# A state-space scan whose skip term is added by TensorE through a diagonal matrix, and gated while it is read from PSUM

## What is computed

```python
xz = x @ in_proj_w
x_in, z = jnp.split(xz, 2, axis=-1)
xc = silu(conv1d(x_in, conv_w) + conv_b)            # u of the scan
dt = softplus(ssm_out[..., -1:] @ dt_w + dt_b)
dA = jnp.minimum(jnp.exp(delta[..., None] * A), 1.0)
dBu = delta[..., None] * Bm[:, :, None, :] * u[..., None]
...
yk = (states * Ck[:, :, None, :]).sum(-1)           # sum over the 16 states
...
return y + u * Dp[None, None, :]                    # the skip term
...
return y * jax.nn.silu(z) @ out_proj_w              # the gate, then the projection
```

## Time and profile before

| | us |
|---|---|
| median of 3 runs | 1558.58 (1555.74, 1558.58, 1558.62) |
| the profiled execution | 1558.36 |
| its span | 1556.6 |
| PE busy | 1307.7 (84%) |
| weight loads on PE busy | 506.7 (33%) |
| VectorE (DVE) busy | 1243.2 (80%) |
| ScalarE (ACT) busy | 1039.3 (67%) |
| GpSimd (POOL) busy | 661.3 (42%) |

### The profile page before, as it was taken

How to read it: one execution, slowest core, us unless ns; L and a number is a source line. 1 busy time by engine, 2 the same in 40 slices (tenths; PEclk the granted TensorE clock), 3 DMA queues, 4 the chain that set the end, 5 groups by cost and what they waited for, 6 DMA issues and landing times.

```text
span 1556.6 us, 22553 instructions
## 1 busy us (share of the span) xinstructions
PE 1307.7 (84%) x8408; PEld 506.7 (33%) x8408; DVE 1243.2 (80%) x1491; ACT 1039.3 (67%) x1821; POOL 661.3 (42%) x609
## 2 busy tenths in 40 slices
PE   4365659976985897888569999999999999999998
PEld 1111224433433343333212222222222222235963
DVE  0889988999899786456679999999999999943522
ACT  3542357755853663445239998999899988997653
POOL 0678867986787684744503112111111113111430
PEclk9666789997996998999759999999999999999999
DMA  7122213322321221223212011100010000000210
GB/s 219 66 65 81 68 49 96 88 69 75 81 75 54 81 75 31 55 68 50 33 54 50 29 29 48 22 2 2 2 23 2 2 2 19 6 26 13 75 31 27
DMA packets 63696, 75.71 MB, mean 49 GB/s; under 512 B 8633, under 2 KB 39226, under 8 KB 63458
## 3 DMA queue, kind: packets, MB, share of 16 engines
q1 hardware_dynamic: 62818, 72.70, 17.2%
q0 software_dynamic: 768, 1.57, 0.3%
HBM read 66.04 MB, written 8.21 MB: 48 GB/s over the span
## 4 chain that ended last, share of the span: by engine, by line
PE 44%; DVE 28%; issue 12%; POOL 11%; ACT 4%; DMA 1%; SPq 1%; DVEq 0%; POOLq 0%; ACTq 0%
DVE mx L1641 16%; PE PS L952 11%; PE PS L940 6%; PE PS L909 4%; DVE D L1430 3%; POOL D L1881 3%; PE PS L732 3%; PE PS L723 3%; PE PS L1024 2%; PE PS L1039 2%; DVE PS L1416 2%; POOL D L1897 2%; PE PS L1060 2%; PE PS L1048 2%; DVE PS L1422 2%
## 5 line engine op out<-in xcount | busy, mean ns | idle before, releaser
L1304 ACT ACTIVATE aa<-PS 128x512 f32<-128x512 f32 x1024 | 551.6, 598 | 57.6 <-PE PS L940 46.7
L1641 DVE TENSOR_REDUCE mx<-PS 128x2 f32<-128x1024 f32 x480 | 552.5, 1218 | 7.9 <-PE PS L909 5.1
L952 PE MATMUL PS<-aa,D 128*32 128x256 f32 x4096 | 321.6, 391 | 1.6 <-ACT aa L1304 0.6
L940 PE MATMUL PS<-D 54*128 54x512 bf16 x1024 | 212.0, 390 | 9.5 <-ACT aa L1304 8.9
L909 PE MATMUL PS<-D 51*128 51x512 bf16 x960 | 190.0, 385 | 17.5 <-DVE mx L1641 16.9
L1995 POOL CAST n<-nm 4x512 bf16<-4x512 f32 x15 | 9.0, 602 | 446.2 <-ACT nm L1286 446.2
L1416 DVE TENSOR_TENSOR_SCAN PS<-PS,D 128x512 f32<-128x512 f32 x128 | 157.5, 1230 | 10.3 <-POOL D L1897 3.5
L1194 ACT ACTIVATE HB<-PS 128x512 f32<-128x512 f32 x144 | 84.6, 596 | 114.9 <-PE PS L732 114.0
L732 PE MATMUL PS<-xnT,f_w 128*128 128x512 f32 x288 | 157.8, 641 | 2.4 <-ACT HB L1194 1.8
L1167 ACT ACTIVATE D<-D,Am 128x512 f32<-128x512 f32 x128 | 85.1, 713 | 97.8 <-DVE D L1430 95.9
L952 PEld LDWEIGHTS PS<-aa,D 128*32 128x32 f32 x4096 | 84.2, 108 | 191.9 <-issue 152.9
(11 more groups left out here) (326 smaller groups left out, 1771.2 us busy)
## 6 DMA issues: line engine op xcount, KB each, us to landing
D<-bc SPq DMA_DIRECT2D x128, 256.0 KB, 3.6
GB<-gd SPq DMA_DIRECT2D x32, 256.0 KB, 4.6
D<-sc SPq DMA_DIRECT2D x72, 64.0 KB
aa<-in_L_ffn_W SPq DMA_DIRECT2D x9, 256.0 KB, 3.4
D<-in_L_ffn_W SPq DMA_DIRECT2D x9, 256.0 KB, 3.5
f_w<-in_L_ffn_experts_w SPq DMA_DIRECT2D x1, 2048.0 KB, 9.3
f_w<-in_L_ffn_experts_w SPq DMA_DIRECT2D x8, 256.0 KB, 6.0
aa<-gh SPq DMA_DIRECT2D x1, 2048.0 KB, 9.3
```

The source lines that it names most:

```text
L940: e.matmul(take_exp(s + hh), KS[64 * hh:64 * hh + 54, p, 128 * kb:128 * kb + 128], QP[64 * hh:64 * hh + 54, qc % 2, p, :], start=True, sto ...
L952: t = e.matmul(PS[32 * j:32 * j + 32, 7, cs], va[:, kb, 9 * h:9 * h + 32], Pt[K % 3][:, 512 * j + 256 * n:512 * j + 256 * n + 256], start= ...
L1304: e.activation(Pt[K % 3][:, c:c + 512], bank((s + hh) % 3), ACT.Exp).then_inc(S("e_free"), 1)
L1641: e.tensor_reduce(mx4[:, G % 2, b, 2 * pair:2 * pair + 2, c:c + 1], max_banks(m), AX.X, ALU.max).then_inc(freed(m)[0], 1)
```

## The change

The skip term `u * D` is added on TensorE. A new tile `skip` holds for each half a diagonal matrix with D on its diagonal, made once at the start by GpSimd (two operations on 128x128, behind the table `rank`, and ahead of the first `delta * u`). In `sums` at n = 9, behind the identity matmul of each half, one more matmul adds `skip[g] * U[g]` to the same bank: two per chunk, eight in all. `collect` on VectorE now reads the bank and multiplies it by the gate in one operation per half; the two gating operations of `epilog` are gone, eight in all. The semaphore `yz` goes; who waited for it waits for `y`.

```diff
@@ -451,6 +451,8 @@
             w_al = sa("w_al", [128, 2, 16])
             w_D = sa("w_D", [128, 2])
             w_out = sa("w_out", [128, 2, 128])
+
+            skip = sa("skip", [128, 2, 128])
             Am = sa("Am", [128, 32])
             f_w1 = sa("f_w1", [128, 9, 512])
             f_w2 = sa("f_w2", [128, 9, 4, 128])
@@ -676,11 +678,15 @@
                         w.wait_ge(S("y"), 2 * (tc - 1) + g + 1)
                     e.matmul(bank(g), ident[:, :], wb[k % 4][:, g, :], start=(n == 0), stop=(n == 15)).then_inc(
                         S("mm_sum"), 1)
+                    if n == 9:
+                        w.wait_ge(S("p_u"), 2 * tc + 2)
+                        w.wait_ge(S("tables"), 10)
+                        e.matmul(bank(g), skip[:, g, :], U[tc % 3][:, g, :], start=False, stop=False)
 
             def epilog(tc):
                 Ux = U[tc % 3]
                 yield
-                w.wait_ge(S("yz"), 2 * tc + 2)
+                w.wait_ge(S("y"), 2 * tc + 2)
                 w.wait_ge(S("x_ffn"), tc)
                 for j in range(4):
                     for g in range(2):
@@ -1130,7 +1136,7 @@
                     yield
                 for g in range(2):
                     w.wait_ge(S("p_mm_z"), 2 * tc + g + 1)
-                    w.wait_ge(S("yz"), 2 * (tc - 2))
+                    w.wait_ge(S("y"), 2 * (tc - 2))
                     e.activation(Zx[:, g, :], bank(7), ACT.Silu).then_inc(S("p_z"), 1)
                     yield
                 yield
@@ -1432,20 +1438,15 @@
                                      op1=ALU.add).then_inc(S("sX"), 1)
 
             def collect(tc):
-                Ux = U[tc % 3]
+                Ux, Zx = U[tc % 3], ZS[tc % 3]
                 for g in range(2):
                     w.wait_ge(S("mm_sum"), 2 * (16 * tc + 15) + g + 1)
                     w.wait_ge(S("p_du"), 2 * tc + g + 1)
-                    e.scalar_tensor_tensor(out=Ux[:, g, :], in0=Ux[:, g, :], scalar=w_D[:, g:g + 1], in1=bank(g),
-                                           op0=ALU.mult, op1=ALU.add).then_inc(S("y"), 1)
+                    w.wait_ge(S("p_z"), 2 * tc + 2)
+                    e.scalar_tensor_tensor(out=Ux[:, g, :], in0=bank(g), scalar=1.0, in1=Zx[:, g, :], op0=ALU.mult,
+                                           op1=ALU.mult).then_inc(S("y"), 1)
 
             def epilog(tc):
-                Ux, Zx = U[tc % 3], ZS[tc % 3]
-                for g in range(2):
-                    w.wait_ge(S("y"), 2 * tc + g + 1)
-                    w.wait_ge(S("p_z"), 2 * tc + 2)
-                    e.scalar_tensor_tensor(out=Ux[:, g, :], in0=Ux[:, g, :], scalar=1.0, in1=Zx[:, g, :], op0=ALU.mult,
-                                           op1=ALU.mult).then_inc(S("yz"), 1)
                 yield from idle(4 + behind(tc))
                 xs = x_tok[:, 4 * tc:4 * tc + 4, :].rearrange("p b d -> p (b d)")
                 w.wait_ge(S("mm_out"), tc + 1)
@@ -1855,6 +1856,9 @@
                 power(0, 0, "p")
                 for x in range(8):
                     e.memset(rank[:, :, x], 8.0 - x).then_inc(S("tables"), 1)
+                w.wait_ge(S("d_scan"), W_SCAN)
+                for g in range(2):
+                    e.tensor_scalar(skip[:, g, :], ident[:, :], w_D[:, g:g + 1], None, ALU.mult).then_inc(S("tables"), 1)
                 for g in range(2):
                     w.wait_ge(S("p_dl"), g + 1)
                     w.wait_ge(S("p_u"), g + 1)
```

## The result

The changed kernel takes 1561.91 us (median of 17 runs, 1560.46 to 1563.93), the kernel before, beside it on the same chip, 1558.16 us (17 runs, 1555.74 to 1560.85). The ratio is 1.0027, with a 95% interval of 1.0020 to 1.0035: 4.2 us slower (3.1 to 5.5). The forecast was 1561.1. It had called "no change" the likeliest outcome (0.45) and "slower" the second (0.38); by its own bound of 1561.7 the kernel is slower, by 0.2 us, and the interval leaves out no change. The profiled execution took 1562.13 us, its span is 1560.4.

A forecast was written before the change was run, and what follows sets the result against it. VectorE was taken to set the pace where matmuls are few, TensorE where the feed-forward part runs. Matmuls +4.9, end of chunk 2 −2.0 and of chunk 3 −0.2 gave +2.7 us on 1558.36: 1561.1 us, range 1555.5 to 1564.0.

The forecast's parts named there:

- its own bound of 1561.7: Whole kernel: about 0.2% (3.1 us) can be told from no change; above 1561.7 us is slower, below 1555.5 faster.
- The eight matmuls, +4.9 us: Feed-forward stretches: TensorE has no slack, so skip matmuls cost 1.6, 1.6 and 1.7 us in chunks 1, 2, 3.
- Ends of chunks 0 and 1, 0 us: Removed gating pairs save nothing: VectorE waits longer for ScalarE's softplus, whose chain the pair is not in.
- the 1.9 forecast: Sign at the end of chunk 1: VectorE's softplus wait of 0.59 us grows by 1.3 to 1.9 us.
- not 4.7: Sign at the end of chunk 0: VectorE's softplus wait of 3.40 us grows by 1.3 to 4.7 us.
- case E: Rival: the granted clock falls otherwise; one prolog convolution group at the other level is worth 2.75 us either way; chance 0.12.
- End of chunk 2, −2.0 us: No prolog left: the removed pair, which held VectorE 1.9 us beside GpSimd's clamp, gains 1.9, and `collect` 0.1 us.
- case D: Rival: nothing gained; at chunk 2's end VectorE meets another wait, or a GpSimd collision returns elsewhere; 1563.3 us, chance 0.13.
- End of chunk 3, −0.2 us: The pair's 1.29 us mostly lost: the cast behind it, starting earlier, is held by GpSimd's unmoved memset; 0.2 us gained.
- the 1.4 that the forecast named as its sign: End of chunk 3: the cast behind the last `collect` takes about 1.4 us.
- Its other sign, last sums ahead of 604 us: End of chunk 3: the forecast is wrong if the last sums come earlier than at 604 us.
- The forecast of +2.7: Whole kernel: 4.9 − 2.0 − 0.2 = +2.7 us on the profiled 1558.36 us, giving 1561.1; chance 0.52.

The follow-up runs named there:

- pe_only: The kernel before plus eight extra matmuls at n = 9 against a matrix of zeros, VectorE's operations kept: 1572.19 us, ratio 1.0031 to the kernel before.
- skip_n3: The changed kernel with the skip matmuls at n = 3 instead of n = 9: 1563.69 us, ratio 0.9983 to the kernel before.
- dve_only: The changed kernel without the skip matmuls, so u * D is left out of the result: 1563.39 us, ratio 0.9983 to the kernel before.
- n3_memset: The changed kernel with skip matmuls at n = 3 and GpSimd's first key memset behind VectorE's casts: 1561.13 us, ratio 0.9976 to the kernel before.
- filler2: The changed kernel plus unread matmuls in both TensorE gaps at the ends of chunks 0 and 1: 1566.78 us, ratio 1.0020 to the kernel before.
- filler: The changed kernel plus three unread matmuls in TensorE's 3.9 us gap ending chunk 0's and 1's feed-forward parts: 1564.09 us, ratio 0.9997 to the kernel before.
- before_again: The kernel before, unedited, run for a second profile on the second chip, where the kernel before takes 1564.88 us (23 runs).

## Why the prediction was right, and where it was not

**The eight matmuls, +4.9 us: right.** pe_only shows 1.6, 1.6 and 1.7 at the three gates, and measured +4.9 (2.7 to 7.2) in all. The reason was the right one as well: a stretch with 36.00 of 36.00 us of TensorE, and a wait of VectorE for it at the end. skip_n3 takes the same matmuls out of these stretches and turns +4.2 us into −2.7.

**Ends of chunks 0 and 1, 0 us: right in amount; at chunk 0 it was another wait.** At chunk 1 dve_only, n3_memset and filler2 lose again by step 38 the 1.1 to 1.2 us that the missing pair gave, and the wait for softplus is longer by that: 1.69 instead of 0.59 in filler2, near the 1.9 forecast. At chunk 0 that wait stayed (3.42 against 3.40, not 4.7). VectorE was stopped earlier, by a wait of 0.88 us for the output projection (L1453 at 198.88), which stood behind the prolog's matmuls on TensorE. I had looked for an operation of VectorE that TensorE waits for, and overlooked that VectorE would come too early for what TensorE brings next.

**The granted clock, case E: in the list with its size and a chance of 0.12, but not in the sum.** The changed kernel loses 2.5 us in the prolog group at the end of chunk 1, beyond those 1.2, on three chips; case E had priced it at 2.75. filler2 shows the cause by taking it away: with two of TensorE's gaps filled the clock stays at 2.4 GHz, the group takes 3.70 us again, and the steps lose 2.7 us less. The kernel before has a half-clock stretch there too (0.51 from 318 to 325 us), but it is over before the group, as the clock of 1.00 from 326 us shows. What in the change makes it longer stays open. dve_only and pe_only both keep the group at 3.70 us, so in their profiles neither half does it alone; in the changed kernel the gap of 3.90 us ends at 319.26 and the clock is back only after 329.

By the Trainium skill's page TensorE: Matmul & The Clock Gate, section Part 1: The HAM clock gate, the clock follows TensorE's recent work, and keeping it busy holds the clock up. filler2 agrees (1.00 and 3.70 us, against 0.50 and 6.18), and so does filler, in which a gap of 2.03 us was left (0.51 and 5.33 us).

**End of chunk 2, −2.0 us: the mechanism was right, the size was given back in part.** From step 48 to 51 the steps gain 1.7 us in dve_only and 1.6 in n3_memset. The changed kernel keeps 0.9: ScalarE's copies of TensorE's combined weights came late, and VectorE waited 0.67 and 0.69 us for them at L1543 and L1540, one of the places that case D names. Behind this, too, stands the granted clock. Two of the matmul groups that these weights come from, in the changed kernel:

```profile
465.84 1.40 PE L779 MATMUL PS<-w_convq,w_Wq 128*128 128x384 f32 x2
475.83 1.49 PE L773 MATMUL PS<-w_kproj,w_convk 128*128 128x128 f32 x6
```

They took 0.81 and 0.89 us before, and from 470 to 477 us the clock was 0.53 here and 0.87 before. pe_only, whose two groups took 1.49 and 1.48 us, shows a wait of 1.45 us at the first of these places; dve_only, with 0.81 and 1.01, shows none.

Another gain, 0.4 us in the changed kernel and 0.8 to 0.9 in dve_only and n3_memset, lies between steps 56 and 57. It is not the pair's, since pe_only, which keeps the pair, has it too (0.9). There VectorE waits for TensorE at the first gate of chunk 2's feed-forward part; from the first up matmul to that gate it took 32.88 us at a clock of 0.84 before, and 31.98 us at 0.86 in pe_only. So of the 1.3 us that the changed kernel shows from 48 to 57, 0.9 are the term that was forecast at 2.0.

**End of chunk 3, −0.2 us: the term that failed.** "The memset starts at the last sums, as the second `collect` does, so it stays where it is." It did not stay. In dve_only and skip_n3 the step holds to the tenth (the cast 1.50 us, 0.2 us gained, and n3_memset frees it by moving the memset). But in all seven kernels with matmuls at n = 9, pe_only among them, the six records of the key convolution ahead of the last sums ran at the full clock. In the changed kernel TensorE's timeline has

```profile
601.94 2.74 PE L802 MATMUL PS<-xnT,w_convk 128*128 128x512 f32 x6
604.52 1.88 PE L679 MATMUL PS<-wb,ident 128*128 128x512 f32 x4
```

where the kernel before has this (timeline, and its stretch from 598 to 602 us, to be held against the one above):

```profile
597.76 4.44 PE L796 MATMUL PS<-xnT,w_convk 128*128 128x512 f32 x6
602.04 1.88 PE L677 MATMUL PS<-wb,ident 128*128 128x512 f32 x4
598.00:602.00 4.00, 4.00 (x6) 1.54 (x5) 3.86 (x7) 0.00 (x0) 0.00 (x0) 0.57 0.02 4
```

The sums and with them the memset came 1.7 us earlier against VectorE, the last `collect` no longer waited, and 1.9 us were gained instead of 0.2. The cast took 0.53 us, not the 1.4 that the forecast named as its sign. Its other sign, last sums ahead of 604 us, did not show, since the steps were 4.2 us late by then: the sums ended at 606.40, against 603.92 before. The clock took 2.5 us at one place and gave 1.7 back at another; the forecast had held it fixed at both.

So the sum reads, in the changed kernel's profile: a start that is 1.5 us earlier (at step 28 the kernels lie between −1.6 and +0.4, not explained; 1.0 of the 1.5 is there by step 5), +4.9 − 0.1 for the matmuls, −1.6 + 3.8 around the end of chunk 1, −1.3, −1.9, in all +2.3 at the casts. Another 1.6 us are lost between 1350 and 1400 us, where the clock was 0.90 instead of 1.00 for a moment, and the profile ends 3.8 us later. The forecast of +2.7 lies 1.5 below the measured +4.2. Among the terms that it missed are +2.5 (the prolog group), +1.1 (end of chunk 2) and −1.7 us (end of chunk 3); that it came so near is in part luck, since they have both signs.

## What to carry to other kernels

Before moving work to another engine, read which engine has no gap in the very stretch where it will land, and place it elsewhere if the order allows: the same eight matmuls cost some 4.9 us at one state of a chunk and nothing that could be measured at another. Work taken from an engine is worth what lies before its next wait, and each freed operation asks what it will now run beside or arrive too early for. Where TensorE has short gaps ahead of a group on the critical path, write down the granted clock of that group as a term of its own: here it moved by 2.5 us in a group that the change did not touch. And where a median moves by less than its runs spread, as with filler2, read the steps of the traces before calling a cause shown.

## What was not expected of the hardware

On all three later chips every profile, of the kernel before too, has a stop of several engines at once between 1307 and 1330 us, which neither profile of the first chip has. In before_again (timelines of TensorE and VectorE, then the stretches):

```profile
1318.56 0.61 PE L940 MATMUL PS<-D 54*128 54x512 bf16 x1 [3.39 <-issue]
1319.32 1.23 DVE L1641 TENSOR_REDUCE mx<-PS 128x2 f32<-128x1024 f32 x1 [4.38 <-remote]
```

```profile
1310.00:1320.00 10.00, 5.57 (x44) 1.38 (x42) 5.41 (x7) 5.59 (x11) 7.56 (x9) 0.90 0.16 52
1320.00:1330.00 10.00, 9.40 (x80) 2.66 (x80) 8.77 (x10) 6.82 (x13) 0.51 (x1) 0.75 0.03 8
```

The clock falls behind it, and the two together cost that profile 6.4 us (7 to 9 in the others). That is about what lies between the median of the kernel before on the first chip and its medians on the others (6.2 to 8.1 us). The profile names no releaser for TensorE here ("issue"); in the four profiles of the chip of pe_only it names ScalarE. The cause stays open. What it teaches is to compare only kernels that ran on the same chip, and to use the steps of two traces up to such a place.

A cast whose operands are both in SBUF takes 1.50 us beside GpSimd's memset and 0.42 without it, and ends 0.28 to 0.29 us behind the memset's end in dve_only and skip_n3, while a fused product with one operand in PSUM keeps its time beside the same memset (in dve_only at most 691 ns, median 681).

By the Trainium skill's page SBUF — State Buffer, section Who interferes with whom, a copy or cast of VectorE in one of its fast modes uses a pair of ports that it shares with GpSimd, and the instruction that comes second waits until the first is done. The trace agrees, in dve_only as before: the cast that started beside the memset ended just behind it.
